# One transformer block on one core: the last row's down tiles, value sums and output turns are put in another order

## The chip, the cores and the metric

The kernel runs on one core of a Trainium2 chip. The metric is the device time of one execution in microseconds (us); less is better. A core has five engines with a queue of instructions each, which run side by side and meet only through semaphores: TensorE (PE in the profile: matmuls, with weight loads as PEld), VectorE (DVE), ScalarE (ACT), GpSimd (POOL), and SyncE (SP), which here only issues DMA transfers.

## The reference

```python
xn = layernorm(x)                              # x is (16, 512, 512)
q, k, v = split(xn @ w_qkv.T + b_qkv)          # 16 heads of 32
attn = softmax(causal(q @ k.T / sqrt(32)))
a = (attn @ v) @ w_out.T + b_out
f = (silu(xn @ gate_w.T * gate_s) * (xn @ up_w.T * up_s)) @ down_w.T * down_s   # hidden width 1408
return x + a + f
```

The sixteen rows of the batch (512 tokens each) are independent. Here a "row" is one of these sixteen.

## The kernel before

All weights stay in SBUF. Every operand that float16 can't hold is split into a high and a low float16 half, so a product takes three matmul groups (high by high, low by high, high by low) where both sides are split, and two where the weights are ternary.

**Tiles.** A row has four token tiles of 128 tokens. Attention is done in 20 chunks (`NCH`), two to each unit of `UNITS`. A unit is a query tile of a group of four heads: `U3` is token tile 3, `U20` tiles 2 and 0, `U1` tile 1 of two head groups at once. The first ten chunks belong to head groups 0 and 1, the last ten to groups 2 and 3. The last unit is a `U1`, so chunks 18 and 19 hold only token tile 1 of head groups 2 and 3; every other part of the attention output is finished by chunk 17.

**Slots.** `period(b, mode)` on each engine runs a row in 20 slots. In slot s, PE computes scores for chunks s and s+1 (if s is even), then two stretches of filling work, the value sums of chunk s-2 (`values`, 16 short matmuls), and a third stretch of filling. DVE takes the row maxima of chunk s (`bank_max`, L1155), ACT the exponents (L855) and the high half (`p_hi`, L865), POOL the low half (`p_lo`, L1244), SP turns both halves with two DMA transposes (L506 high, L508 low) into `p_t`, and PE can then sum the values two slots later. What comes out is summed and normalised on DVE (L1163, L1167, L1173), split into `o_hl` on ACT (L873, `o_hi`) and POOL (L1249, `o_lo`).

**The filling work** is written out by hand in `PLAN`, one string per slot: `d1*4` is four parts of down tile 1, `g` and `u` are gate and up tiles, `q k v` projections of the input, `o` a tile of the output projection of the row before. A down tile (`down_part`) has six parts of 4, 4, 4, 4, 3 and 3 matmuls, 22 in all; an output projection tile (`project`) has three parts of 4. Words 0-1, 2-3 and the rest of a string go to the three stretches of the slot. Results take one of three PSUM banks in turn (`bank_free` waits until the bank's last user was read). `DVE_MID`, `ACT_MID` and `POOL_MID` say in the same way in which slot and place each engine takes the results.

**Row ends.** In a row's slot 18 SP turns the attention output of head groups 0 and 1 (`turn_o(0)`, `turn_o(1)`, L456); groups 2 and 3 are turned in slot 2 of the next row, whose slots 4 and 5 hold the projection. The modes are `first` (row 0), `mid` (a hardware loop over rows 1 to 14), `last` (row 15) and `tail` (what is left of row 15). Before the change, `last` uses `PLAN` without the items of a next row, and `tail` has 7 slots with the output projection alone. In the tail, SP first issues the load of row 15's input as the residual (L472) and turns groups 2 and 3 when all 20 chunks are done. POOL adds the output bias to the residual in four tiles (`b0` to `b3`, L1253) and the scaled down product (`f0` to `f3`, L1259), DVE adds the projection (`combine`, L1088), and SP stores each tile.

The tail of POOL's table begins with these two slots, in which `o_lo` of chunks 18 and 19 stands ahead of the third place:

```python
POOL_MID = [
    "| | b0 b1", "| | b2 b3", "| | f0 f1", "| | f2 f3", ...
```

Of the kernel before, what the change touches and what calls it, by code (L numbers as in the profile page):

```python
# [7 lines left out]
F16 = mybir.dt.float16  # L8
# [5 lines left out]
P = 128  # L14
B, S, D = 16, 512, 512
H, HD = 16, 32
# [60 lines left out]
PLANS = {"none": PLAN_NONE, "first": PLAN_FIRST, "mid": PLAN, "last": PLAN, "tail": PLAN}  # L77
PARTS = dict(v=3, q=3, k=3, r=3, s=3, g=2, u=2, o=3, d=6)
# [3 lines left out]
def has(mode, kind):  # L82
    if kind in "obf":
        return mode != "first"
    if kind in "rsyYxRnl":
        return mode in ("first", "mid")
    return mode != "tail"


TAIL_SLOTS = 7  # L90
# [79 lines left out]
READS = dict(DVE=(DVE_MID, DVE_FIRST), ACT=(ACT_MID, ACT_FIRST), POOL=(POOL_MID, POOL_FIRST))  # L170
# [3 lines left out]
def read_places(engine, mode):  # L174

    places = {}
    for s, text in enumerate(READS[engine][mode == "first"]):
# [82 lines left out]
def block_program(nc, x, w_qkv, gate, up, w_out, down, smalls, b_out, down_s, out):  # L260
    with ExitStack() as ctx:
# [16 lines left out]
        o_hl = sb("o_hl", [P, DC, 2, TT, P], F16)  # L278
# [33 lines left out]
        o_t = region_a[:, :].rearrange("p (c w n) -> p c w n", c=DC, w=2)  # L312
# [39 lines left out]
        def o_dst(s, w):  # L352

            kind, g = UNITS[s // 2]
            cols = slice(2 * HD * (s % 2), 2 * HD * (s % 2) + 2 * HD)
            if kind == "U3":
                return o_hl[:, g, w, 3:4, cols].rearrange("p t (j d) -> p j t d", d=HD)
            if kind == "U20":
                return o_hl[:, g, w, 0:3:2, cols].rearrange("p t (j d) -> p j t d", d=HD)
            return o_hl[:, g:g + 2, w, 1, cols].rearrange("p e (j d) -> p j e d", d=HD)  # L360
# [32 lines left out]
        consts_done = ctx.enter_context(nc.semaphore("consts_done"))  # L393
        bv_split = ctx.enter_context(nc.semaphore("bv_split"))
# [18 lines left out]
        def row_of(b, kind):  # L413
            return b - 1 if kind == "o" else b + 1 if kind in "rs" else b
# [5 lines left out]
        def _(sp):  # L420
# [34 lines left out]
            def turn_o(c, name):  # L455
                sp.dma_start_transpose(o_t[:, c, :, :].rearrange("p w (t n) -> p (w t) n", n=P),  # L456
                                       o_hl[:, c, :, :, :].rearrange("p w t n -> p (w t n)"))\
                  .then_inc(sem[name], 16)

            def period(b, mode):  # L460
                cur, prev, nxt = mode != "tail", mode != "first", mode in ("first", "mid")
                for s in range(NCH if cur else TAIL_SLOTS):
# [15 lines left out]
                    if s in (5, 6) and prev:  # L478
                        for t in range(2 * (s - 5), 2 * (s - 5) + 2):
                            sp.wait_ge(sem["out_added"], at(b - 1, "out_added", t + 1))  # L480
# [37 lines left out]
        def _(pe):  # L518
# [57 lines left out]
            def project(bank, t, k):  # L576
                a, v = [(0, 0), (1, 0), (0, 1)][k]
                toks = slice(t * P, (t + 1) * P)
                for c in range(DC):
                    last = mm(ps[:, bank, :], o_t[:, c, v, toks], weight(OUT, a, c, 0, D),  # L580
                              k == 0 and c == 0, k == 2 and c == DC - 1)
                if k == 2:
                    last.then_inc(sem["proj_ready"], 1)

            def bank_free(b, mode, n):

                user, ago = bank_user(mode, n)
                if user is None:
                    return
                kind, i = user  # L590
                r = row_of(b - ago, kind)
                if kind == "v":
                    pe.wait_ge(sem["v_lo"], at(r, "v_lo", V_COUNT[i]))
                elif kind == "g":
                    pe.wait_ge(sem["gated"], at(r, "gated", i + 1))
                elif kind == "u":
                    pe.wait_ge(sem["hidden"], at(r, "hidden", i + 1))
                elif kind == "o":
                    pe.wait_ge(sem["out_added"], at(r, "out_added", i + 1))
                elif kind == "d":  # L600
# [84 lines left out]
            def period(b, mode):  # L685
                cur, prev, nxt = mode != "tail", mode != "first", mode in ("first", "mid")

                def fill(s, place):
                    for n, k in PLACED[mode].get((s, place), []):
# [26 lines left out]
                        elif kind == "u":  # L716
                            ffn_part(bank, UP, i, k, "up_ready", mode != "first" or i >= UNFLAGGED)
                        elif kind == "d":
                            down_part(b, bank, i, k)
                        else:  # L720
# [178 lines left out]
        def _(dve):  # L899
# [164 lines left out]
            def period(b, mode):  # L1064
# [14 lines left out]
                def scale_down(bank, t):  # L1079
                    dve.wait_ge(sem["down_ready"], at(b, "down_ready", t + 1))  # L1080
# [4 lines left out]
                def combine(bank, t):  # L1085
                    dve.wait_ge(sem["proj_ready"], at(b - 1, "proj_ready", t + 1))
# [5 lines left out]
                def take(s, place):  # L1092
                    for kind, i in READ_PLACES["DVE", mode][s, place]:
# [8 lines left out]
                        elif kind == "d":  # L1102
                            scale_down(bank_at(mode, kind, i), i)
# [94 lines left out]
        def _(pool):  # L1198
# [35 lines left out]
            def period(b, mode):  # L1234
# [16 lines left out]
                def add_bias(t):  # L1251
                    pool.wait_ge(sem["res_loaded"], at(b - 1, "res_loaded", 16))
# [9 lines left out]
                def take(s, place):  # L1262
                    for kind, i in READ_PLACES["POOL", mode][s, place]:
# [8 lines left out]
                        elif kind == "b":  # L1272
                            add_bias(i)
# [51 lines left out]
```

## Time and profile before

| | us |
|---|---|
| median of 3 runs | 1969.26 (1968.77 to 1971.07) |
| the profiled execution | 1970.23 |
| its span, first to last instruction | 1968.5 |
| PE busy | 1894.2 (96% of the span) |
| DVE, ACT, POOL busy | 1347.6, 1294.5, 1361.9 |
| mean granted TensorE clock | 0.988 of full speed |

Busy times are of the profiled execution. What lies around its span is 1.7 us.

### The profile page before, as it was taken

How to read it: one execution, taken by the hardware profiler on the slowest of the kernel's cores; microseconds unless marked ns; L12 is line 12 of the kernel's file. 1: busy time of each engine (PE TensorE's matmuls, PEld its weight loads, DVE VectorE, ACT ScalarE, POOL GpSimd, SP SyncE). 2: the span in 40 equal slices, each digit the busy share in tenths (PEclk: the TensorE clock that was granted, in tenths of full speed). 3: DMA queues.
4: the chain of work that ended last, by engine and by line, in shares of the span. 5: the costliest groups of instructions: out<-in, count | busy, mean ns of one | idle time of the engine just before them, and what ended most of it. 6: DMA issues, size and time to landing. Idle time of an engine off the chain costs nothing.

```text
span 1968.5 us, 48427 instructions
## 1 busy us (share of the span) xinstructions
PE 1894.2 (96%) x15624; PEld 913.2 (46%) x15624; DVE 1347.6 (68%) x3925; ACT 1294.5 (66%) x2315; POOL 1361.9 (69%) x1097
## 2 busy tenths in 40 slices
PE   5879999999999999999999999999999999999995
PEld 2334444444444444444444444444444444444442
DVE  7896676767667676666767666676766767676663
ACT  3776666766667666766766666676676767666662
POOL 1186686766868677687866768676676867668754
PEclk9899999999999999999999999999999999999997
DMA  9248868596776869768586876859677685977855
GB/s 336 38 77 141 156 108 152 112 160 141 121 150 115 152 128 151 145 116 154 109 160 124 153 143 110 158 103 162 134 129 149 116 149 118 157 142 120 149 91 111
DMA packets 840049, 267.89 MB, mean 136 GB/s; under 512 B 812864, under 2 KB 812864, under 8 KB 839232
## 3 DMA queue, kind: packets, MB, share of 16 engines
q1 hardware_dynamic: 839872, 265.15, 71.7%
q8 instruction: 158, 2.59, 0.6%
q14 instruction: 19, 0.16, 0.0%
HBM read 46.94 MB, written 16.78 MB: 32 GB/s over the span
## 4 chain that ended last, share of the span: by engine, by line
PE 80%; DVE 5%; POOL 5%; issue 4%; SPq 3%; DMA 2%; ACT 1%; DVEq 0%; POOLq 0%; ACTq 0%
PE ps L520 80%; POOL phl L1244 2%; DMA p_t<-phl 2%; SPq L442 1%; POOL region_b L1222 1%; DVE memory L938 1%; DVE p L1155 1%; POOL memory L1239 1%; SPq L506 1%; SPq L508 0%; POOL region_a L1227 0%; DVE hidden_tmp L1069 0%; SPq L456 0%; POOL rstd L1218 0%; DVE hidden_tmp L1075 0%
## 5 line engine op out<-in xcount | busy, mean ns | idle before, releaser
L520 PE MATMUL ps<-x_t,memory 128*128 128x512 f16 x4384 | 1004.8, 381 | 9.2 <-DVE memory L938 4.2
L1244 POOL TENSOR_TENSOR phl<-p,phl 128x1024 f16<-128x1024 f32 x320 | 683.0, 2135 | 456.5 <-ACT phl L865 456.4
L855 ACT ACTIVATE p<-p,nmax 128x384 f32<-128x384 f32 (+3 forms) x1024 | 530.1, 557 | 288.7 <-DVE nmax L1155 269.3
L520 PEld LDWEIGHTS ps<-x_t,memory 128*128 128x128 f16 x4384 | 408.0, 98 | 504.7 <-issue 58.3
L1155 DVE CUSTOM_DVE_ANT_0 p<-ps,causal,cst 128x384 f32<-128x384 f32 (+3 forms) x1024 | 515.4, 547 | 97.1 <-PE ps L520 77.0
L865 ACT CAST phl<-p 128x1024 f16<-128x1024 f32 x320 | 334.0, 1044 | 38.4 <-DMA p_t<-phl 22.4
L520 PE MATMUL ps<-memory 128*128 128x512 f16 x1408 | 323.4, 380 | 0.8 <-DVE bout_bc L1007 0.8
L1239 POOL TENSOR_TENSOR memory<-hidden_tmp,memory 128x512 f16<-128x512 f32 x176 | 204.0, 1159 | 69.2 <-ACT memory L827 69.2
L1163 DVE TENSOR_REDUCE ps<-ps 128x132 f32<-128x264 f32 (+1 forms) x320 | 122.0, 381 | 164.0 <-PE ps L520 163.9
L520 PEld LDWEIGHTS ps<-vv,p_t 128*128 128x128 f16 x5120 | 186.8, 96 | 93.0 <-issue 17.4
L520 PE MATMUL ps<-vv,p_t 128*128 128x68 f16 (+1 forms) x5120 | 193.7, 185 | 13.2 <-DMA p_t<-phl 13.0
L520 PEld LDWEIGHTS ps<-memory 128*128 128x128 f16 x1408 | 131.4, 98 | 154.9 <-issue 7.0
L873 ACT CAST o_hl<-o 128x128 f16<-128x128 f32 (+1 forms) x320 | 87.8, 274 | 163.2 <-DVE o L1173 162.3
L520 PE MATMUL ps<-memory,region_a 128*128 128x512 f16 x768 | 176.1, 383 | 10.2 <-DMA region_a<-o_hl 10.2
L1069 DVE SCALAR_TENSOR_TENSOR hidden_tmp<-hidden_tmp,ps 128x512 f32<-128x512 f32 x176 | 120.1, 682 | 86.8 <-ACT hidden_tmp L820 86.3
L520 PE MATMUL ps<-memory,x_t 128*128 128x512 f16 x768 | 173.3, 379 | 0.0
L1025 DVE SCALAR_TENSOR_TENSOR qk<-ps,smalls_in,qk 128x512 f16<-128x512 f32 x128 | 96.0, 750 | 95.5 <-ACT qk L764 95.4
L820 ACT ACTIVATE hidden_tmp<-ps,tanh_scale 128x512 f32<-128x512 f32 x176 | 119.4, 679 | 51.3 <-PE ps L520 46.1
L520 PE MATMUL ps<-qk 32*128 32x128 f16 (+3 forms) x3072 | 134.3, 298 | 5.9 <-DVE nmax L1155 5.9
L764 ACT ACTIVATE qk<-ps,smalls_in 128x512 f16<-128x512 f32 x128 | 87.2, 681 | 75.6 <-PE ps L520 75.6
L1249 POOL TENSOR_TENSOR o_hl<-o,o_hl 128x128 f16<-128x128 f32 (+1 forms) x320 | 125.8, 393 | 11.6 <-ACT o_hl L873 11.6
L1075 DVE SCALAR_TENSOR_TENSOR hidden_tmp<-hidden_tmp,h_scale,ps 128x512 f32<-128x512 f32 x176 | 130.8, 743 | 2.1
(78 smaller groups left out, 1318.6 us busy)
## 6 DMA issues: line engine op xcount, KB each, us to landing
region_b<-x SPq DMA_DIRECT2D x32, 1024.0 KB, 5.8
out<-region_b SPq DMA_DIRECT2D x64, 256.0 KB, 2.5
p_t<-phl SPq DMA_TRANSPOSE x640, 3.1
memory<-w_qkv SPq DMA_DIRECT2D x3, 1024.0 KB, 9.1
memory<-down SPq DMA_DIRECT2D x1, 2816.0 KB, 22.0
memory<-gate SPq DMA_DIRECT2D x1, 2560.0 KB, 9.6
memory<-up SPq DMA_DIRECT2D x1, 2560.0 KB, 16.5
x_t<-region_a SPq DMA_TRANSPOSE x64, 4.0
```

Of the source, the lines that this page charges most:

```text
L520: return nc.tensor.matmul(o, lhsT=l, rhs=r, start=start, stop=stop, skip_group_check=True)
L820: nc.scalar.activation(hidden_tmp[:, f % 2, :], ps[:, bank, :], ACT.Tanh, scale=tanh_scale[:, f:f + 1]).then_inc(sem["tanh_done"], 1)
L855: last = nc.scalar.activation(cols, cols, ACT.Exp, scale=-1.0, bias=nmax[:, s % 2, i:i + 1])
L865: nc.scalar.copy(phl[:, s % 2, 0, :], p32[:, s % 2, :]).then_inc(sem["p_hi"], 1)
L1025: v.scalar_tensor_tensor(out=qk[:, t, side, 1, :], in0=ps[:, bank, :], scalar=bqkv[:, tile:tile + 1], in1=qk[:, t, side, 0, :], op0=ALU.ad ...
L1069: v.scalar_tensor_tensor(out=hidden_tmp[:, f % 2, :], in0=hidden_tmp[:, f % 2, :], scalar=1.0, in1=ps[:, bank, :], op0=ALU.add, op1=ALU.mu ...
L1075: v.scalar_tensor_tensor(out=hidden_tmp[:, f % 2, :], in0=hidden_tmp[:, f % 2, :], scalar=h_scale[:, f:f + 1], in1=ps[:, bank, :], op0=ALU ...
L1155: v.tensor_tensor_reduce(p32[:, s % 2, col:col + w], ps[:, 2 * (s % 2) + jj, col - 512 * jj:col - 512 * jj + w], causal[:, S - w:S], cst[: ...
L1163: v.tensor_reduce(o_sums(n), o_halves(n), AX, ALU.add).then_inc(sem["o_sum"], 1)
L1239: g.tensor_tensor(h_t(1, f), hidden_tmp[:, f % 2, :], h_t(0, f), ALU.subtract)\
L1244: g.tensor_tensor(phl[:, s % 2, 1, :], p32[:, s % 2, :], phl[:, s % 2, 0, :], ALU.subtract)\
L1249: g.tensor_tensor(o_dst(s, 1), o_src(s), o_dst(s, 0), ALU.subtract).then_inc(sem["o_lo"], 1)
```

## The change

1. `PLAN_LAST`: the last row makes down tiles 0 and 1 only, in slots 14 to 19, with 2 parts in each slot where there were 4 to 6. Down tiles 2 and 3 become items `D` of the tail.
2. `PLAN_TAIL`: the tail has three slots instead of seven. Slot 0 is all of D2 and the first part of D3 (the first 16 matmuls of D2 ahead of the value sums of chunk 18). Slot 1 is D3's parts 1 to 4, the value sums of chunk 19, D3's part 5 and projection tile 0. Slot 2 is projection tiles 2, 3 and 1.
3. `o_hl` and `o_t` are laid out by token tile first and half second, with the tiles in the order 0, 2, 3, 1, in all rows. In the tail, groups 2 and 3 are turned in two steps: tiles 0, 2, 3 as soon as chunk 17 is split, tile 1 once chunk 19 is. Only projection tile 1 waits for the second step. The other rows turn whole groups as before.
4. Row 15's residual load moves from the tail to slot 8 of the last row, and the four bias additions (`c0` to `c3`) to POOL's slots 10 to 13.
5. DVE scales d0 in slot 17 and d1 in slot 19; D2 and D3 follow the outputs of chunks 18 and 19. POOL's tail is `f0 f1`, o_lo of chunk 18, `f2`, o_lo of chunk 19, `f3`.

```diff
+PLAN_LAST = PLAN[:14] + ["u10*2 d0*2", "d0*2", "d0*2", "d1*2", "d1*2", "d1*2"]
+PLAN_TAIL = ["D2*6 D3*1", "D3*5 o0*3", "o2*3 o3*3 o1*3"]
+PLANS = {"none": PLAN_NONE, "first": PLAN_FIRST, "mid": PLAN, "last": PLAN_LAST, "tail": PLAN_TAIL}
+TILE_ORDER = [0, 2, 3, 1]
-TAIL_SLOTS = 7
+TAIL_SLOTS = len(PLAN_TAIL)
...
+DVE_LAST = DVE_MID[:16] + ["| | |", "d0 | | |", "| | |", "| | | d1"]
+POOL_LAST = list(POOL_MID)
+POOL_LAST[10:14] = [text + f" c{t}" for t, text in enumerate(POOL_MID[10:14])]
+DVE_TAIL = ["| | | D2", "| | | D3", "o0 o2 o3 o1 | | |"]
+ACT_TAIL = ["| | | |"] * 3
+POOL_TAIL = ["f0 f1 | | f2", "| | f3", "| |"]
...
-        o_hl = sb("o_hl", [P, DC, 2, TT, P], F16)
+        o_hl = sb("o_hl", [P, DC, TT, 2, P], F16)
...
+            def turn_o_tiles(tiles, done):
+
+                for c in (2, 3):
+                    sp.dma_start_transpose(o_t[:, c, tiles, :, :].rearrange("p t w n -> p (t w) n"),
+                                           o_hl[:, c, tiles, :, :].rearrange("p t w n -> p (t w n)"))\
+                      .then_inc(done, 16)
...
-                    if s == 0 and prev:
-                        if cur:
-                            sp.wait_ge(sem["ln_lo"], at(b, "ln_lo", TT))
-                        else:
-                            sp.wait_ge(sem["out_stored"], at(b - 2, "out_stored", 16 * TT))
+                    if s == 0 and prev and cur:
+                        sp.wait_ge(sem["ln_lo"], at(b, "ln_lo", TT))
                         sp.dma_start(res[:, :, :], x[b - 1].rearrange("(t p) n -> p t n", p=P))\
                           .then_inc(sem["res_loaded"], 16)
-                    if s == 2 and prev:
+                    if s in (0, 1) and not cur:
+                        sp.wait_ge(sem["o_lo"], at(b - 1, "o_lo", NCH - 2 + 2 * s)).then_inc(wait_over["sp"], 1)
+                        if s == 0:
+                            turn_o_tiles(slice(0, TT - 1), sem["turned23"])
+                        else:
+                            turn_o_tiles(slice(TT - 1, TT), turned_last)
+                    if s == 2 and prev and cur:
...
+                    if s == 8 and cur and prev and not nxt:
+                        sp.wait_ge(sem["out_stored"], at(b - 1, "out_stored", 16 * TT))
+                        sp.dma_start(res[:, :, :], x[b].rearrange("(t p) n -> p t n", p=P))\
+                          .then_inc(sem["res_loaded"], 16)
...
+                            elif i == 1 and k == 0 and not cur:
+                                pe.wait_ge(turned_last, 32)
                             project(bank, i, k)
```

## Rows read from the trace of the kernel before

**Rows 1.** Engines by stretch: start:end, length, busy times (instructions), granted clock, DMA share, GB/s.
```profile
1709.00:1817.00 108.00, 107.74 (x893) 51.90 (x892) 74.36 (x222) 72.21 (x133) 80.08 (x64) 1.00 0.73 134
...
1911.00:1921.77 10.77, 10.77 (x99) 5.28 (x98) 5.94 (x19) 5.92 (x11) 5.83 (x5) 1.00 0.70 100
...
1931.98:1938.42 6.44, 0.60 (x16) 0.52 (x17) 1.02 (x4) 1.29 (x2) 2.75 (x3) 0.63 0.99 191
```

**Rows 2.** TensorE in order of time: start, length, what, idle before it.
```profile
1910.34 5.34 PE L520 MATMUL ps<-memory 128*128 128x512 f16 x24
...
1917.36 0.83 PE L520 MATMUL ps<-qk 32*128 32x128 f16 x24
...
1924.62 0.60 PE L520 MATMUL ps<-vv,p_t 128*128 128x68 f16 x16
...
1928.12 3.18 PE L520 MATMUL ps<-memory 128*128 128x512 f16 x14
1931.98 0.60 PE L520 MATMUL ps<-vv,p_t 128*128 128x68 f16 x16 [0.68 <-DMA p_t<-phl]
1938.42 0.84 PE L520 MATMUL ps<-vv,p_t 128*128 128x68 f16 x16 [5.84 <-DMA p_t<-phl]
1940.96 0.84 PE L520 MATMUL ps<-vv,p_t 128*128 128x68 f16 x16 [1.70 <-DMA p_t<-phl]
1951.98 13.27 PE L520 MATMUL ps<-memory,region_a 128*128 128x512 f16 x48 [10.18 <-DMA region_a<-o_hl]
```

**Rows 3.** SyncE's queue in order of time: start, length of issuing, what.
```profile
1928.36 2.20 SPq L508 DMA_TRANSPOSE p_t<-phl  x1
1930.75 2.60 SPq L456 DMA_TRANSPOSE region_a<-o_hl  x2
...
1937.69 1.28 SPq L508 DMA_TRANSPOSE p_t<-phl  x1
1939.03 0.57 SPq L472 DMA_DIRECT2D region_b<-x  x1
1947.39 2.62 SPq L456 DMA_TRANSPOSE region_a<-o_hl  x2
```

**Rows 4.** The chain that ended last: start, length, what.
```profile
1934.89 3.40 DMA p_t<-phl
```

**Rows 5.** GpSimd in order of time, slot 15 and the tail.
```profile
1914.86 2.12 POOL L1244 TENSOR_TENSOR phl<-p,phl 128x1024 f16<-128x1024 f32 x1 [0.58 <-ACT phl L865]
...
1940.69 0.43 POOL L1249 TENSOR_TENSOR o_hl<-o,o_hl 128x128 f16<-128x128 f32 x1 [5.14 <-ACT o_hl L873]
1944.43 2.48 POOL L1253 TENSOR_TENSOR region_b<-region_b,bout_bc 128x512 f32<-128x512 f32 x2 [3.31 <-DMA region_b<-x]
1946.87 0.43 POOL L1249 TENSOR_TENSOR o_hl<-o,o_hl 128x128 f16<-128x128 f32 x1
```

**Rows 6.** Engines by stretch, as Rows 1, for the clock.
```profile
1933.50:1951.98 18.48, 1.68 (x33) 1.50 (x34) 1.93 (x7) 0.89 (x3) 10.02 (x10) 0.50 0.70 154
1951.98:1957.40 5.42, 5.42 (x13) 1.87 (x14) 0.10 (x1) 0.00 (x0) 2.63 (x3) 0.50 0.00 0
1957.40:1965.30 7.90, 7.84 (x36) 3.38 (x34) 2.17 (x4) 0.00 (x0) 0.00 (x0) 0.99 0.26 100
...
103.50:107.50 4.00, 3.95 (x11) 1.50 (x12) 4.00 (x8) 1.04 (x3) 3.06 (x2) 0.58 0.95 102
117.50:121.00 3.50, 2.33 (x24) 1.29 (x24) 3.43 (x6) 3.45 (x6) 2.23 (x2) 1.00 0.31 61
```

**Rows 7.** VectorE in order of time, slots 15 and 17.
```profile
1912.87 0.08 DVE L1155 DVE_READ_ACCUMULATOR2_ANT nmax<- 128x1 f32 x1
...
1924.83 0.75 DVE L1081 SCALAR_TENSOR_TENSOR ffn_out<-ps,cst,downs_bc 128x512 f32<-128x512 f32 x1 [0.49 <-PE ps L520]
```

**Rows 8.** TensorE early in row 0, two waits.
```profile
103.55 5.30 PE L520 MATMUL ps<-x_t,memory 128*128 128x512 f16 x16 [3.03 <-DVE lo_flag L933]
...
117.71 1.89 PE L520 MATMUL ps<-x_t,memory 128*128 128x512 f16 x8 [1.93 <-DVE hidden_tmp L1069]
```

More of the change, by code:

```diff
@@ L76 @@
 ]
-PLANS = {"none": PLAN_NONE, "first": PLAN_FIRST, "mid": PLAN, "last": PLAN, "tail": PLAN}
-PARTS = dict(v=3, q=3, k=3, r=3, s=3, g=2, u=2, o=3, d=6)
+PLAN_LAST = PLAN[:14] + ["u10*2 d0*2", "d0*2", "d0*2", "d1*2", "d1*2", "d1*2"]
+PLAN_TAIL = ["D2*6 D3*1", "D3*5 o0*3", "o2*3 o3*3 o1*3"]
+PLANS = {"none": PLAN_NONE, "first": PLAN_FIRST, "mid": PLAN, "last": PLAN_LAST, "tail": PLAN_TAIL}
+PARTS = dict(v=3, q=3, k=3, r=3, s=3, g=2, u=2, o=3, d=6, D=6)
+TILE_ORDER = [0, 2, 3, 1]
 def has(mode, kind):
@@ L84, in has @@
         return mode != "first"
+    if kind == "D":
+        return mode == "tail"
     if kind in "rsyYxRnl":
@@ L87, in has, with o_rank @@
     return mode != "tail"
-TAIL_SLOTS = 7
+TAIL_SLOTS = len(PLAN_TAIL)
+def o_rank(mode, t):
+    return TILE_ORDER.index(t) if mode == "tail" else t
 BEFORE = {"first": "none", "mid": "mid", "last": "mid", "tail": "last"}
@@ L169 @@
 ]
-READS = dict(DVE=(DVE_MID, DVE_FIRST), ACT=(ACT_MID, ACT_FIRST), POOL=(POOL_MID, POOL_FIRST))
+DVE_LAST = DVE_MID[:16] + ["| | |", "d0 | | |", "| | |", "| | | d1"]
[4 more added lines that the diff above has]
+POOL_TAIL = ["f0 f1 | | f2", "| | f3", "| |"]
+TABLES = {
+    "first": dict(DVE=DVE_FIRST, ACT=ACT_FIRST, POOL=POOL_FIRST), "mid": dict(DVE=DVE_MID, ACT=ACT_MID, POOL=POOL_MID),
+    "last": dict(DVE=DVE_LAST, ACT=ACT_MID, POOL=POOL_LAST), "tail": dict(DVE=DVE_TAIL, ACT=ACT_TAIL, POOL=POOL_TAIL),
+}
 STEPS = dict(DVE=4, ACT=5, POOL=3)
@@ L176, in read_places @@
     places = {}
-    for s, text in enumerate(READS[engine][mode == "first"]):
+    for s, text in enumerate(TABLES[mode][engine]):
         parts = text.split("|")
@@ L413, in row_of @@
         def row_of(b, kind):
-            return b - 1 if kind == "o" else b + 1 if kind in "rs" else b
+            return b - 1 if kind in "oD" else b + 1 if kind in "rs" else b
         def qk_count(kind, t):
@@ L455, in turn_o @@
             def turn_o(c, name):
[L456 to L457 removed]
+                sp.dma_start_transpose(o_t[:, c, :, :, :].rearrange("p t w n -> p (t w) n"),
+                                       o_hl[:, c, :, :, :].rearrange("p t w n -> p (t w n)"))\
                   .then_inc(sem[name], 16)
+            def turn_o_tiles(tiles, done):
[3 more added lines that the diff above has]
+                      .then_inc(done, 16)
             def period(b, mode):
@@ L477, in period @@
                         turn_o(3, "turned23")
-                    if s in (5, 6) and prev:
-                        for t in range(2 * (s - 5), 2 * (s - 5) + 2):
-                            sp.wait_ge(sem["out_added"], at(b - 1, "out_added", t + 1))
+                    if s in ((5, 6) if cur else (1, 2)) and prev:
+                        half = s - (5 if cur else 1)
+                        for n in range(2 * half, 2 * half + 2):
+                            t = n if cur else TILE_ORDER[n]
+                            sp.wait_ge(sem["out_added"], at(b - 1, "out_added", n + 1))
                             sp.dma_start(out[b - 1].rearrange("(t p) n -> p t n", p=P)[:, t, :], res[:, t, :])\
                               .then_inc(sem["out_stored"], 16)
+                    if s == 8 and cur and prev and not nxt:
+                        sp.wait_ge(sem["out_stored"], at(b - 1, "out_stored", 16 * TT))
+                        sp.dma_start(res[:, :, :], x[b].rearrange("(t p) n -> p t n", p=P))\
+                          .then_inc(sem["res_loaded"], 16)
                     if s == 8 and nxt and prev:
@@ L577, in project @@
                 a, v = [(0, 0), (1, 0), (0, 1)][k]
-                toks = slice(t * P, (t + 1) * P)
                 for c in range(DC):
-                    last = mm(ps[:, bank, :], o_t[:, c, v, toks], weight(OUT, a, c, 0, D),
+                    last = mm(ps[:, bank, :], o_t[:, c, TILE_ORDER.index(t), v, :], weight(OUT, a, c, 0, D),
                               k == 0 and c == 0, k == 2 and c == DC - 1)
@@ L590, in bank_free @@
                 kind, i = user
-                r = row_of(b - ago, kind)
+                r, m = row_of(b - ago, kind), BEFORE[mode] if ago else mode
                 if kind == "v":
```

33 lines of the change are left out of this document (19 added, 14 removed).

## The prediction

> **What bounds the kernel now.** I read the stretches first. In a whole row of the loop TensorE is busy 107.74 of 108 us [rows 1]: a row costs what its matmuls cost, and the new layout of `o_hl` and `o_t` changes the size of no instruction there (each write keeps its strides and count, each turn its 1024 columns, each weight load its 128 contiguous columns), so rows 0 to 14 are costed at nothing, and TensorE's fullness would hide small differences. What can change is the end. I took TensorE in order of time next [rows 2]: it works without a gap until slot 18 [rows 1, 2], then waits 0.68, 5.84 and 1.70 us for the turned probabilities of chunks 17, 18 and 19 and 10.18 us for the turned output: 18.4 us in which it has nothing to do, although 22 of the down matmuls of slots 18 and 19 (d3) could have stood there, and d2's too. Third, the chain and the two queues that feed those waits. SyncE issues six transposes back to back between 1930.75 and 1939.0 [rows 3], with the DMA engines 0.99 busy [rows 1], and a transpose lands 3.4 us after it is issued [rows 4]. Then it loads the residual; GpSimd waits 3.31 us for that load and adds two bias tiles before it splits chunk 19 [rows 5], so the last turns leave at 1947.39 [rows 3]; with chunk 18's time from the start of its values to its split, 2.7 us, they could have left at 1943.7. Last, the clock: from 1933.5 on TensorE is granted half speed (1.2 GHz instead of 2.4), and keeps it for the first 5.4 us of the projection [rows 6].
>
> **Unit prices.** 24 down matmuls take 5.34 us and 14 take 3.18 [rows 2], so one costs 0.216 us at full clock. The 48 of the projection took 13.27 us where 48 x 0.216 is 10.4: the half clock cost 2.9 us there. A `values` is 0.60 us at full clock and 0.84 at half [rows 2].
>
> **Step 1, slots 14 to 19 with 44 matmuls fewer.** That is 9.5 us of TensorE, but only what the attention's own chain leaves open can be won. In slot 15 TensorE now has 8 matmuls after 1910.34 instead of 24: it is at the values of chunk 13 at 1912.1 and done at 1912.7. The scores of chunks 16 and 17 also need the maxima of chunk 15, read at 1912.87 to 1912.95 [rows 7], so they start at 1913.05 instead of 1917.36 [rows 2]: 4.3 us earlier. From here TensorE no longer sets the pace. The low half of chunk 15 is made by GpSimd from 1914.86 to 1916.98 [rows 5], as before; turned and landed 3.4 us later that is 1920.45, so the values of chunk 15 run at 1920.5 instead of 1924.62: 4.1 earlier. Chunks 16 and 17 pass through the same operations with the same lengths; d0's scaling (0.75 us [rows 7]) now stands ahead of chunk 17's maxima, where d2's stood behind them, which costs a few tenths. I take the low transpose of chunk 17 at 1924.55 instead of 1928.36 [rows 3]: 3.8 us earlier. Behind it SyncE has the same six transposes at the same spacing, so chunk 17's values run at 1928.2 and chunk 18's at 1934.6 instead of 1938.42 [rows 2]. Step 1 is worth 3.8 us, not 9.5. From below: nothing, if the transposes of slots 16 to 18 crowd one another; from above 4.3.
>
> **Step 2, down tiles 2 and 3 in the waits.** After chunk 17's values at 1928.8 TensorE does 16 matmuls of D2 (3.5 us), is done at 1932.3 and waits until 1934.6; these are free. After chunk 18's values (to 1935.2) come 25 matmuls, 5.4 us, before the values of chunk 19, which start at 1940.6. Their data would be there at 1940.96 - 3.8 = 1937.2, so here work is put ahead of a value sum that was ready, by 3.4 us. It costs nothing as long as tile 1's turn is not late: TensorE is then simply busy. The values end at 1941.2; 3 more matmuls of D3, 0.65, and the projection can start at 1941.9, if tiles 0, 2 and 3 are turned. Their turn needs only chunk 17 and follows chunk 19's low transpose, at 1933.9 + 1.3; two transposes of 2.6 us together [rows 3] and the landing give about 1940. In time by almost 2 us.
>
> **Step 3, the projection.** 48 matmuls at full clock are 10.4 us: it ends at 1952.25 instead of 1965.26. Tile 1 is last, at 1941.9 + 36 x 0.216 = 1949.7. From the start of a value sum to its split is 2.7 us (1938.42 to 1941.12 [rows 2, 5]), so chunk 19 is split at 1943.3; at the full-size price for its two small transposes (1947.39 to 1951.98 is 4.6 us [rows 2, 3]) they land at 1947.9. In time by 1.8 us. GpSimd has `f0 f1` done before chunk 18 comes and `f2` (1.2 us, after D2's scaling) between 18 and 19, so o_lo of chunk 19 waits for nothing. Behind SyncE's wait for it stand only the stores, which are needed later.
>
> **Step 4, the residual's load and bias.** In slot 8 the load waits for the stores of slots 5 and 6, with the probabilities' transposes queued behind; every row of the loop does this with the next input, and TensorE stays full [rows 1]. The four additions are 1.24 us each [rows 5] in slots where the loop's rows also have the normalisation, so they are hidden; without that cover 5 us. The end behind the last matmul (3.2 us) does not change.
>
> **Sum at full clock.** 1965.26 - 1952.25 = 13.0 us: 3.8 of step 1; 6.3 between chunk 18's values and the projection (13.6 us before, now 0.6 + 5.4 + 0.6 + 0.65 = 7.3); 2.9 in the projection itself.
>
> **The clock.** The last 2.9 us are the doubtful part. TensorE will be thinner than before: the slots from 15 on hold 8 down matmuls per 4 us, with waits of some 2.8 us before chunk 17's values and 2.3 before chunk 18's. After a wait of 3.03 us early in the kernel the clock was at half (0.58 over the next 4 us), after one of 1.93 us it stayed at 1.00 [rows 6, 8]; here the waits lie between. A drop in slots 17 to 19 costs almost nothing, as half-speed matmuls only fill the waits. A drop that lasts past 1934.6 costs up to what the projection paid, 2.9. I take half, 1.3, as both neighbours are equally near; the ends are 0 and 2.9. The Trainium skill (TensorE: Matmul & The Clock Gate, HAM oscillation) speaks against this change here: short bursts of matmuls with waits for data between them are throttled again at each wait, and every burst starts cold. By it the sum would be 10.1 instead of 11.7; the early rows agree with it for one wait and not for the other.
>
> So 11.7 us less. The profiled execution (span and 1.7 us around it) would be 1970.23 - 11.7 = 1958.5; the median of the runs lies 0.97 below that execution, so **1957.6**.
>
> **Rivals.**
> - **A, the clock stays low into the projection.** For: the waits above, and the drop at 1933.5, only 0.9 us after chunk 17's values. Gain 13.0 - 2.9 = 10.1, time 1959.2; this lies in the forecast's own range.
> - **B, the slots keep their old pace.** Step 1 gives nothing because SyncE's transposes, not TensorE, set the slots. For: 2.20 us for issuing one at 1928.36 [rows 3], where the one at 1937.69 took 1.28, and the six in a row. Against: TensorE was full in slots 15 and 16 and its value sums waited for no DMA there [rows 1, 2]. Gain 9.2, with the clock low 6.3: 1960.1 to 1963.
> - **C, tile 1's turn is late.** The value sum of chunk 19 is held behind 15 matmuls of D3. If splitting and turning took 9.1 us instead of 7.3, the projection would wait. At worst another 2 us: gain 9.7, 1959.6.
> - **D, slower.** TensorE, thinned in slot 15, falls to half clock and stays there to the end. From slot 15 it has 8 + 6 + 22 + 44 + 48 = 128 long matmuls, 0.21 us dearer each: 27 us on TensorE, of which the waits in the slots take 7 or so and the rest exceeds the gain of 13.0 by 7: 1976. It decides from 62 half-clock matmuls on the path. Against: a full 5.4 us brought the clock back [rows 6], and cold matmuls would fill the slots.
> - **E, no effect.** The projection waits as long as before because something else holds its turn, e.g. the residual's load. Against: the load is gone from the tail, the order of SyncE's queue is plain.
>
> **Chances.** The forecast, with the clock nearer to full speed than to A, 0.42; A 0.30; B 0.12; C 0.06; D 0.03; E 0.03; more than 13.5 gained (issue gaps that shrink) 0.04. The forecast's own range is 1956.2 to 1959.2. Two in ten left out: 1955.0 to 1962.0. 0.2% is 3.9 us, about what a measurement of this kernel can tell from no change: faster by more than that 0.94, within it 0.03, slower 0.03.
>
> **What would show it.** Right: values of chunk 15 some 4 us earlier, chunk 18's near 1934.6, the D matmuls without idle time between chunk 18's values and the projection's last matmul, that one near 1952 to 1955. Wrong: idle time of TensorE before the projection or before its last 12 matmuls (C); the spacing of slots 16 to 18 as before (B); matmuls of 0.43 us through D3 and most of the projection (A, D). A difference in the loop's rows would mean that the layout is not neutral.

## The result, and the profile after

The changed kernel takes 1955.2 us (median of 4 runs, 1953.38 to 1956.67) against 1970.16 for the kernel before, timed beside it: ratio 0.9922, with a 95% interval of 0.9905 to 0.994. That is 15.4 us less, with 11.8 to 18.7 inside the interval. Forecast were 11.7 us, with 7.3 to 14.3 as the range that follows from its two ends: the direction was right, and the gain lies above that range, where the prediction ("more than 13.5 gained") had put a chance of 0.04. In time, 1955.2 us lies below the forecast's own range of 1956.2 to 1959.2. Where the gain came from is mostly as forecast; what was missed is told by terms further down.

Runs of one kernel differ by up to 6.5 us. The traces, one execution of each kernel, show where such differences can arise: in the twelve of them, row 1 starts to turn its probabilities at 192.9 to 195.6 us, and from there to slot 14 of the last row it is 1710.1 to 1714.6 us, so time differs both while the weights are prepared and in the loop. (For the kernels before and after, it is 1711.1 and 1711.2.) In what follows I therefore use a second measure, the **end stretch**: from the start of the scores of chunks 14 and 15 of the last row (the last place up to which all kernels do nearly the same) to the end of the span. It is one execution per kernel too. Before: 1968.5 - 1905.67 = 62.8 us. After: 1954.6 - 1906.58 = 48.0. So the end gained 14.8 us in the profiled executions, and this one reached slot 14 0.9 us later than the one before.

TensorE in order of time in the changed kernel, beside [rows 2]:

```profile
1906.58 0.83 PE L562 MATMUL ps<-qk 32*128 32x512 f16 x12
...
1914.01 0.84 PE L562 MATMUL ps<-qk 32*128 32x128 f16 x24 [0.43 <-DVE nmax L1200]
...
1921.42 0.60 PE L562 MATMUL ps<-vv,p_t 128*128 128x68 f16 x16 [2.12 <-DMA p_t<-phl]
...
1923.35 2.86 PE L562 MATMUL ps<-memory 128*128 128x512 f16 x8
...
1928.29 0.60 PE L562 MATMUL ps<-vv,p_t 128*128 128x68 f16 x16 [0.24 <-DMA p_t<-phl]
1928.74 3.61 PE L562 MATMUL ps<-memory 128*128 128x512 f16 x16
1933.88 0.60 PE L562 MATMUL ps<-vv,p_t 128*128 128x68 f16 x16 [1.53 <-DMA p_t<-phl]
1934.33 5.55 PE L562 MATMUL ps<-memory 128*128 128x512 f16 x25
1939.72 0.61 PE L562 MATMUL ps<-vv,p_t 128*128 128x68 f16 x16
1940.17 0.81 PE L562 MATMUL ps<-memory 128*128 128x512 f16 x3
1940.82 10.52 PE L562 MATMUL ps<-memory,region_a 128*128 128x512 f16 x48
```

From chunk 18's values (1933.88) on TensorE has no gap: D2, D3, the values of chunk 19 and all four projection tiles stand end to end. The waits of 5.84, 1.70 and 10.18 us before [rows 2] are one of 1.53. In the thinned slots ahead TensorE now has waits that were not there, the longest of 2.12 us. The projection takes 10.52 us where it took 13.27.

The engines by stretch, beside [rows 1, 6]:

```profile
1709.00:1817.00 108.00, 107.94 (x904) 52.25 (x903) 73.49 (x220) 72.55 (x132) 80.16 (x64) 1.00 0.72 135
1921.90:1925.30 3.40, 3.40 (x34) 1.49 (x31) 2.37 (x11) 1.89 (x5) 2.39 (x2) 0.50 1.33 126
1925.30:1933.90 8.60, 6.83 (x59) 3.14 (x58) 4.14 (x17) 4.89 (x10) 5.26 (x5) 1.00 0.97 188
1933.90:1951.40 17.50, 17.44 (x108) 8.20 (x108) 5.51 (x12) 0.60 (x2) 5.53 (x6) 1.00 0.51 96
```

The row of the loop is as full as before. The clock did fall, behind the wait of 2.12 us, and stood at half for the scores and 8 down matmuls of slot 18; it was back before the tail, where it stayed at 1.00.

SyncE's queue, beside [rows 3], and the chain that ended last, beside [rows 4]:

```profile
1924.70 1.38 SPq L550 DMA_TRANSPOSE p_t<-phl  x1
1926.27 2.61 SPq L482 DMA_TRANSPOSE region_a<-o_hl  x2
1929.06 1.23 SPq L548 DMA_TRANSPOSE p_t<-phl  x1
1930.41 1.26 SPq L550 DMA_TRANSPOSE p_t<-phl  x1
1931.86 1.23 SPq L548 DMA_TRANSPOSE p_t<-phl  x1
1933.38 1.23 SPq L550 DMA_TRANSPOSE p_t<-phl  x1
1934.73 10.00 SPq L489 DMA_TRANSPOSE region_a<-o_hl  x4
```

```profile
1924.70 3.46 DMA p_t<-phl
...
1930.41 3.33 DMA p_t<-phl
...
1933.88 17.48 PE ps L562 x108
```

Measured from the start of the end stretch, chunk 17's low transpose is issued at 18.1 us (22.7 before), the turns of groups 0 and 1 at 19.7 (25.1), chunk 18's values at 27.3 (32.75), the projection at 34.2 (46.3).

### The profile page after: what moved, and what is told of

The parts are those of the page before. It is cut to its first block, busy times and chain, and to the rows that moved or that the text cites. A ratio compares the mean times of both kernels' runs of the same rounds, so it can differ in the third digit from the quotient of the medians.

```text
span 1954.6 us, 48431 instructions
## 1 busy us (share of the span) xinstructions
PE 1892.8 (97%) x15624; PEld 912.5 (47%) x15624; DVE 1347.6 (69%) x3925; ACT 1294.4 (66%) x2315; POOL 1362.8 (70%) x1097
## 4 chain that ended last, share of the span: by engine, by line
PE 75%; POOL 7%; DVE 6%; issue 4%; SPq 3%; DMA 2%; ACT 1%; DVEq 0%; POOLq 0%; ACTq 0%
PE ps L562 75%; POOL phl L1289 3%; DMA p_t<-phl 2%; SPq L468 2%; POOL region_b L1267 2%; DVE memory L983 1%; DVE p L1200 1%; POOL memory L1284 1%; SPq L548 1%; DVE hidden_tmp L1114 1%; POOL region_a L1272 1%; POOL rstd L1263 0%; SPq L550 0%; DVE hidden_tmp L1120 0%; DVE vareps L1065 0%
## 5 line engine op out<-in xcount | busy, mean ns | idle before, releaser
L910 ACT CAST phl<-p 128x1024 f16<-128x1024 f32 x320 | 334.0, 1044 | 39.6 <-DMA p_t<-phl 23.4
L562 PE MATMUL ps<-vv,p_t 128*128 128x68 f16 (+1 forms) x5120 | 193.0, 185 | 10.5 <-DMA p_t<-phl 10.4
L865 ACT ACTIVATE hidden_tmp<-ps,tanh_scale 128x512 f32<-128x512 f32 x176 | 119.5, 679 | 52.3 <-PE ps L562 46.3
```

The costliest lines, as they stand in the source:

```text
L562: return nc.tensor.matmul(o, lhsT=l, rhs=r, start=start, stop=stop, skip_group_check=True)
L865: nc.scalar.activation(hidden_tmp[:, f % 2, :], ps[:, bank, :], ACT.Tanh, scale=tanh_scale[:, f:f + 1]).then_inc(sem["tanh_done"], 1)
L910: nc.scalar.copy(phl[:, s % 2, 0, :], p32[:, s % 2, :]).then_inc(sem["p_hi"], 1)
```

## The experiments

Each is read by its end stretch; the ratio to the kernel before, with its interval, stands beside it where there is one; the two kernels without a ratio (more warm-up, chunk 19 first) ran once. A matmul in them is one of 512 columns.

| kernel | end stretch, us | ratio of times |
|---|---|---|
| before | 1968.5 - 1905.67 = 62.8 | |
| before, clock kept | 1966.7 - 1906.45 = 60.2 | 0.9993 [0.9983, 1.0003] |
| before, early residual | 1963.1 - 1903.92 = 59.2 | 0.9978 [0.9968, 0.9987] |
| before, more warm-up | 1970.5 - 1908.69 = 61.8 | |
| changed | 1954.6 - 1906.58 = 48.0 | 0.9922 [0.9905, 0.994] |
| changed, down tiles back | 1959.1 - 1905.87 = 53.2 | 0.9956 [0.9942, 0.997] |
| changed, whole turn | 1962.0 - 1905.78 = 56.2 | 0.9968 [0.9956, 0.9979] |
| changed, late residual | 1954.1 - 1904.56 = 49.5 | 0.995 [0.9935, 0.9966] |
| changed, chunk 19 first | 1959.4 - 1906.99 = 52.4 | |
| changed, d0 behind | 1955.1 - 1907.06 = 48.0 | 0.9933 [0.9918, 0.9948] |
| slots filled | 1952.8 - 1904.27 = 48.5 | 0.993 [0.9917, 0.9944] |
| slots filled, kept warm | 1953.6 - 1907.48 = 46.1 | 0.9925 [0.9911, 0.9938] |

### What the half clock cost before

```diff
+                def junk(n):
+                    pe.wait_ge(sem["s_max"], at(b - 1, "s_max", PIECES_UNTIL[-1]))
+                    for _ in range(n):
+                        mm(ps[:, 0, :], x_t[:, 0, 0, 0:P], weight(QKV, 0, 0, 0, D), True, True)
...
+                    if not cur and s == 0:
+                        junk(24)
+                    if not cur and s == 2:
+                        junk(40)
```

> The kernel before, with 24 + 40 extra matmuls of 512 columns in the tail (into a PSUM bank that nobody reads any more): 24 before the value sums of chunk 18, 40 after those of chunk 19, where TensorE waits 5.8 and 10.2 us. Nothing else changes. The end stretch, from the start of the scores of chunks 14 and 15 of the last row to the last instruction, is 62.8 us before and 48.0 after. Theory (the half clock cost the projection 2.9 us, and the change got that back): the first 12 matmuls of the projection take 0.216 us instead of 0.43, the end stretch is 59.9 to 60.2. Rival (the first matmuls are slow for another reason, such as fetching what the transposes just wrote): 62.8, with the clock shown at full.

The tail of TensorE in this kernel:

```profile
1942.32 9.96 PE L520 MATMUL ps<-memory,x_t 128*128 128x512 f16 x40
1952.92 10.52 PE L520 MATMUL ps<-memory,region_a 128*128 128x512 f16 x48 [0.63 <-DMA region_a<-o_hl]
```

The projection starts at 46.5 us of the end stretch (46.3 before) and takes 10.52 us instead of 13.27. So 2.6 to 2.8 of the 14.8 us are the clock alone, and matmuls that compute nothing win them as well. The ratio to before can't tell 2.6 us from nothing; the trace can.

### The residual's load and bias alone

The edit is step 4 of the change, put on the kernel before.

```diff
-                        else:
-                            sp.wait_ge(sem["out_stored"], at(b - 2, "out_stored", 16 * TT))
...
+                    if s == 8 and cur and prev and not nxt:
+                        sp.wait_ge(sem["out_stored"], at(b - 1, "out_stored", 16 * TT))
+                        sp.dma_start(res[:, :, :], x[b].rearrange("(t p) n -> p t n", p=P))\
+                          .then_inc(sem["res_loaded"], 16)
...
+POOL_LAST[10:14] = [text + f" c{t}" for t, text in enumerate(POOL_MID[10:14])]
+POOL_TAIL = ["| |", "| |"] + POOL_MID[2:]
```

> The kernel before with step 4 alone: the residual's load in slot 8 of the last row, the bias in slots 10 to 13. Theory: chunk 19 is split 3.7 us earlier (GpSimd no longer waits for the load and adds two bias tiles first), the turns and the projection follow, the end stretch is 62.8 - 3.7 = 59.1. Rival (the load in slot 8 delays the turns of the probabilities in the last row, or the addition of the down tiles becomes the wait): 60.5 or more, or TensorE with idle time in slots 8 to 13.

GpSimd and TensorE in the tail:

```profile
1939.21 0.43 POOL L1256 TENSOR_TENSOR o_hl<-o,o_hl 128x128 f16<-128x128 f32 x1 [5.15 <-ACT o_hl L880]
1941.74 0.42 POOL L1256 TENSOR_TENSOR o_hl<-o,o_hl 128x128 f16<-128x128 f32 x1 [2.10 <-ACT o_hl L880]
```

```profile
1946.81 13.05 PE L527 MATMUL ps<-memory,region_a 128*128 128x512 f16 x48 [6.50 <-DMA region_a<-o_hl]
```

Chunk 19 is split 2.5 us behind chunk 18, where before it was 6.2 [rows 5]; TensorE's wait shrinks by 3.7. The other way round, with step 4 taken out of the changed kernel:

```diff
+                    if s == 0 and not cur:
+                        sp.wait_ge(sem["out_stored"], at(b - 2, "out_stored", 16 * TT))
+                        sp.dma_start(res[:, :, :], x[b - 1].rearrange("(t p) n -> p t n", p=P))\
+                          .then_inc(sem["res_loaded"], 16)
...
-POOL_TAIL = ["f0 f1 | | f2", "| | f3", "| |"]
+POOL_TAIL = ["| | b0 b1", "| | b2 b3", "f0 f1 f2 f3 | |"]
```

> The changed kernel with step 4 undone: the residual's load is issued in the tail, ahead of the turns of tiles 0, 2 and 3, and the bias is added in the tail, two tiles behind the split of chunk 18 and two behind that of chunk 19, then the four additions of the down tiles. Theory (with the change TensorE is the bound of the tail, and GpSimd has some slack): what cost 3.6 us in the kernel before costs 0.5 to 2 us here, since only VectorE's last combinations wait for GpSimd; end stretch 48.5 to 50. Rival (the early load is needed for the whole gain): 51.5 or more.

GpSimd's bias add, and TensorE's projection, each in order of time:

```profile
1938.98 2.49 POOL L1297 TENSOR_TENSOR region_b<-region_b,bout_bc 128x512 f32<-128x512 f32 x2 [4.78 <-DMA region_b<-x]
```

```profile
1940.34 10.52 PE L561 MATMUL ps<-memory,region_a 128*128 128x512 f16 x48 [1.50 <-DMA region_a<-o_hl]
```

It costs 1.5 us: the load goes ahead of the turns on the DMA engines, and the projection waits 1.50 us for them (GpSimd's own delay is hidden by the projection; I had expected the cost only there, at VectorE's last additions). Not all of the 1.5 need be the load's: in this trace an instruction fetch also falls into the issuing of the first of those turns, which takes 2.38 us, where in the changed kernel the same one, with a fetch near its end, takes 1.31. The same step is worth 3.6 us on one kernel and 1.5 on the other, so the parts of the change don't add.

### The two down tiles back in the slots, and the turn made whole

```diff
-PLAN_LAST = PLAN[:14] + ["u10*2 d0*2", "d0*2", "d0*2", "d1*2", "d1*2", "d1*2"]
-PLAN_TAIL = ["D2*6 D3*1", "D3*5 o0*3", "o2*3 o3*3 o1*3"]
+PLAN_LAST = PLAN
+PLAN_TAIL = ["", "", "o0*3 o2*3 o3*3 o1*3"]
```

> The changed kernel with down tiles 2 and 3 back in slots 15 to 19 of the last row (the old plan); the turns by token tiles, the order of the projection and the early residual stay. Theory: TensorE fills slots 15 to 19 as before, so the value sums come as late as before; the turns of tiles 0, 2 and 3 are issued right behind the last probabilities and land some 5 us later, the projection starts at 39 us of the end stretch, cold, and takes 13.3: 55.5 in all, so about half of the 14.8 us comes from moving the two tiles. Rival (the turns are what counts, and the tiles only fill time): 50 or less.

```diff
-                        sp.wait_ge(sem["o_lo"], at(b - 1, "o_lo", NCH - 2 + 2 * s)).then_inc(wait_over["sp"], 1)
-                        if s == 0:
-                            turn_o_tiles(slice(0, TT - 1), sem["turned23"])
-                        else:
-                            turn_o_tiles(slice(TT - 1, TT), turned_last)
+                        if s == 1:
+                            sp.wait_ge(sem["o_lo"], at(b - 1, "o_lo", NCH)).then_inc(wait_over["sp"], 1)
+                            turn_o(2, "turned23")
+                            turn_o(3, "turned23")
```

> The changed kernel with groups 2 and 3 turned whole once chunk 19 is split; all else stays, also the 25 down matmuls ahead of the value sums of chunk 19. Theory: the split of chunk 19 is done at 35.6 us of the end stretch, the turns take 4.6, the projection starts at 40.3 instead of 34.2: 54.1, and up to 57 if the clock drops in the 5.5 us wait. Rival (the turn is hidden by the down matmuls anyway): 48 to 49.

The projection on TensorE, in order of time, with the down tiles back and then with the whole turn:

```profile
1943.54 12.34 PE L562 MATMUL ps<-memory,region_a 128*128 128x512 f16 x48 [1.34 <-DMA region_a<-o_hl]
```

```profile
1945.92 12.81 PE L561 MATMUL ps<-memory,region_a 128*128 128x512 f16 x48 [5.85 <-DMA region_a<-o_hl]
```

With the down tiles back, the end is 5.2 us longer than with the change; I expected 7.5. Two things made the difference: the projection came at 37.7 us of the stretch instead of 39, and it lost 1.9 us to the half clock instead of 2.9. With the whole turn it is 8.2 us longer: 5.85 of waiting and 2.3 of clock. So both moves are needed, and each is worth more than its own wait, since the wait also takes the clock down. With the down tiles back, chunk 18's values come at 32.7 us, as in the kernel before, and not at 27.3: moving the tiles out makes the slots end earlier. How much earlier they can end is the next question.

### What sets the slots

I had put d0's scaling on the path, at a few tenths of a microsecond.

```diff
-DVE_LAST = DVE_MID[:16] + ["| | |", "d0 | | |", "| | |", "| | | d1"]
+DVE_LAST = DVE_MID[:16] + ["| | |", "| | | d0", "| | |", "| | | d1"]
```

> The changed kernel with VectorE's scaling of d0 (0.75 us) moved from ahead of chunk 17's maxima to the end of slot 17. Theory (that scaling stands on the chain values of chunk 14, maxima of chunk 17, low half of 17, its turn, and with it all later turns): the low transpose of chunk 17 and the values of chunk 18 come 0.65 us earlier, the end stretch is 47.3. Rival (SyncE's queue or TensorE sets these): 47.95.

Nothing was won: chunk 17's low transpose is issued 18.1 us into the end stretch in both kernels. ScalarE in this kernel shows why:

```profile
1919.33 1.96 ACT L900 ACTIVATE p<-p,nmax 128x128 f32<-128x128 f32 x4
1921.84 1.04 ACT L910 CAST phl<-p 128x1024 f16<-128x1024 f32 x1 [0.55 <-DMA p_t<-phl]
```

and so does its chain:

```profile
1918.47 3.29 DMA p_t<-phl
...
1921.84 1.05 ACT phl L910
...
1922.96 2.14 POOL phl L1289
...
1925.18 1.38 SPq L550
```

Chunk 17's exponents are ready 0.55 us before its high half can be written, because the buffer `phl` is read by chunk 15's transposes until they land. From chunk 15 to chunk 17 the work runs in a ring: high half (1.05), low half (2.14), transpose and landing (3.3), high half two chunks later; with the gaps, 6.7 us (1915.13 to 1921.84 in this kernel). In the changed kernel the chain does run through d0's scaling:

```profile
1917.60 0.31 DVE ps L1208
...
1918.30 0.73 DVE ffn_out L1126
```

But there chunk 17's exponents end and chunk 15's transposes land within 0.1 us of each other, so taking either away alone wins nothing.

### The instruction fetch

Chunk 17's low transpose took 2.20 us to issue before [rows 3] and 1.38 after. In the trace of before, a 16 KB fetch of instructions stands in the DMA queues in that time:

```profile
q8 instruction: 1, 0.02, 3.2%
...
p_t<-phl SPq DMA_TRANSPOSE x1, 3.5
```

(The DMA queues from 1928.5 to 1930.5.) It starts at 1929.06. In the changed kernel it comes at 1923.84, while SyncE waits for the low half, and the issue starts at 1924.70.

```diff
-PE_PAD = 38
+PE_PAD = 52
```

> The kernel before with 52 instead of 38 tiny warm-up matmuls at the very start of TensorE's program, where it waits anyway: 28 instructions more ahead of everything. In the trace of before, the 16 KB fetch of instructions at 1929.06 falls into the issuing of chunk 17's low transpose, which takes 2.20 us; in the changed kernel the fetch falls between two issues and that transpose takes 1.38 us. Theory (the fetch is what makes the issuing long, and its place follows from how many instructions TensorE has run): the fetch comes about 1.5 us earlier against the slots, the issuing of that transpose is 1.3 to 1.8 us instead of 2.20, and the end stretch shortens by the same, to 61.9 to 62.4 from 62.75. Rival (the long issue comes from the transposes in flight, which are the same): 2.2 us and 62.75, wherever the fetch is.

SyncE's queue in this kernel, with the low transposes of chunk 17 and of chunk 19, and then TensorE's projection:

```profile
1931.38 1.82 SPq L508 DMA_TRANSPOSE p_t<-phl  x1
...
1940.33 1.26 SPq L508 DMA_TRANSPOSE p_t<-phl  x1
```

```profile
1954.70 12.60 PE L520 MATMUL ps<-memory,region_a 128*128 128x512 f16 x48 [10.26 <-DMA region_a<-o_hl]
```

The fetch moved by 0.4 us (from 23.4 to 23.0 us into the end stretch), not by 1.5, and the issue became 0.38 shorter. The other 0.6 to 0.7 us of the 1.0 won are the projection's, 12.60 instead of 13.27, that is the clock, and with one trace of each kernel they can't be put down to the edit (see the last section).

Over all twelve kernels the issue of chunk 17's low transpose took 2.20, 2.10, 2.49, 2.23 and 1.82 us with a fetch in it, and 1.23 to 1.40 without one. For the other transposes that is not the whole rule. The twelve end stretches have 230 transposes, 27 of them with a fetch inside the issuing: 19 of these took 1.8 to 2.5 us to issue and 8 only 1.23 to 1.33. In seven of the 8 the fetch came 0.9 us or later into the issue, in the long ones within 0.72; the eighth, with the fetch at 0.65, is met below. Of the 203 others three took 1.59, 1.71 and 2.06 us, each right behind one with a fetch in it, and none of the rest more than 1.43. So no long issue stands without a fetch in it or in the one before, but a fetch does not make every issue long. Which instructions bring the fetch, and why it holds an issue up, is not shown.

### Chunk 19 first

`-*4` leaves the first two places of a slot empty, so that all of D3 follows the value sums.

```diff
-PLAN_TAIL = ["D2*6 D3*1", "D3*5 o0*3", "o2*3 o3*3 o1*3"]
+PLAN_TAIL = ["D2*6", "-*4 D3*6 o0*3", "o2*3 o3*3 o1*3"]
```

> The changed kernel with the value sums of chunk 19 right after D2, ahead of all of D3 (22 matmuls), instead of behind 19 of them. Theory (TensorE is the bound from chunk 18's values on, so a value sum may wait behind down matmuls for nothing): TensorE now waits about 1.1 us for chunk 19's turned halves, and the end stretch is 48.9 to 49.1 instead of 47.95. Rival (the turn of tile 1 was close to being the bound, so an earlier split helps): 47.95 or less.

TensorE around chunk 19's values in this kernel, and then the landing that they wait for, from its chain:

```profile
1934.71 1.46 PE L566 MATMUL ps<-memory 128*128 128x512 f16 x6
1938.80 0.60 PE L566 MATMUL ps<-vv,p_t 128*128 128x68 f16 x16 [2.63 <-DMA p_t<-phl]
1939.24 6.59 PE L566 MATMUL ps<-memory 128*128 128x512 f16 x22
```

```profile
1933.81 4.85 DMA p_t<-phl
```

The direction is as expected and the size is not: 4.4 us instead of 1.1. The wait is 2.63 us because chunk 19's transpose takes 4.85 us from issue to landing, not the 3.3 that I had reckoned with (an instruction fetch falls into that time too; in the changed kernel itself the same transpose took 4.6). Behind the wait the clock is at half: 22 matmuls need 6.4 us up to the projection instead of 4.75. Holding a ready value sum behind down matmuls was therefore not free but right: it hides a late landing and keeps the clock. This is one execution, but both parts can be seen in it: 2.63 us of waiting and 1.7 us of half clock make 4.3 of the 4.4.

### Filling the waits that are left

```diff
-PLAN_LAST = PLAN[:14] + ["u10*2 d0*2", "d0*2", "d0*2", "d1*2", "d1*2", "d1*2"]
-PLAN_TAIL = ["D2*6 D3*1", "D3*5 o0*3", "o2*3 o3*3 o1*3"]
+PLAN_LAST = PLAN[:14] + ["u10*2 d0*2", "d0*2", "d0*2", "d1*4", "d1*2 d2*2", "d2*4"]
+PLAN_TAIL = ["D3*6", "-*4 o0*3", "o2*3 o3*3 o1*3"]
...
-DVE_LAST = DVE_MID[:16] + ["| | |", "d0 | | |", "| | |", "| | | d1"]
-DVE_TAIL = ["| | | D2", "| | | D3", "o0 o2 o3 o1 | | |"]
+DVE_LAST = DVE_MID[:16] + ["| | |", "| | | d0", "| | |", "| | | d1 d2"]
+DVE_TAIL = ["| | | D3", "| | |", "o0 o2 o3 o1 | | |"]
```

> The previous one, and down tile 2 put back into the last row, spread over the places where TensorE still waits: d1 with 4 parts in slot 17, its last 2 and 2 of d2 in slot 18, 4 of d2 in slot 19; the tail has D3 alone, around the value sums of chunk 18, and nothing between the values of chunk 19 and the projection. Theory (after chunk 17's transposes the turns of tiles 0, 2 and 3 are the next bound: issued behind chunk 19's low transpose, landing some 4.6 us later): the projection starts 31.5 to 32.5 us into the end stretch instead of 34.2, with TensorE waiting about 2 us before it; 45.5 to 46.5 in all, and 0.5 to 1.5 more if the clock drops in that wait. Rival (the work in slots 17 to 19 delays the chain itself): 47.5 or more, with chunk 18's values later than 26.7 us.

Of this kernel, SyncE's issue of chunk 18's low transpose, and TensorE's last rows:

```profile
1928.17 2.04 SPq L554 DMA_TRANSPOSE p_t<-phl  x1
```

```profile
1935.05 0.60 PE L566 MATMUL ps<-vv,p_t 128*128 128x68 f16 x16 [0.82 <-DMA p_t<-phl]
1937.33 12.21 PE L566 MATMUL ps<-memory,region_a 128*128 128x512 f16 x48 [1.68 <-DMA region_a<-o_hl]
```

The projection starts at 33.1 us instead of 34.2, later than the 31.5 to 32.5 expected: here the fetch falls into chunk 18's low transpose, which takes 2.04 us. The 1.2 us won are more than lost again to the half clock (12.21 us against 10.52), and the end stretch is 48.5 us, 0.5 longer than with the change and above the 45.5 to 46.5 (at most 1.5 more) expected. Extra matmuls keep it up:

```diff
+                    if not cur and s < 2:
+                        junk(3)
...
+                    if not cur and s == 1:
+                        junk(7)
```

> The kernel with filled slots once more, and 13 extra matmuls of 512 columns in the tail, into a PSUM bank that nobody reads any more: 3 ahead of the value sums of chunk 18, 3 ahead of those of chunk 19 and 7 ahead of the projection, where TensorE waited 0.9, 0.8 and 1.7 us. Theory (the filled kernel won 1.2 us up to the projection and lost 1.7 in it to the half clock): the projection starts 33.1 us into the end stretch as in that kernel, its matmuls take 0.216 us from the first on, and the end stretch is 46.7 to 46.9, 1.1 less than with the change. Rival (the clock falls all the same, or the extra matmuls delay a value sum): 48 or more.

TensorE's last rows in this kernel:

```profile
1938.23 1.67 PE L566 MATMUL ps<-memory,x_t 128*128 128x512 f16 x7
1939.83 10.52 PE L566 MATMUL ps<-memory,region_a 128*128 128x512 f16 x48
```

and SyncE's issue of chunk 18's low transpose, with the DMA queues from 1931.27 to 1932.6:

```profile
1931.27 1.26 SPq L554 DMA_TRANSPOSE p_t<-phl  x1
...
q8 instruction: 1, 0.02, 4.5%
```

The end stretch is 46.1 us, 1.9 less than with the change, and some 0.7 less than expected: the projection starts at 32.35 us, not 33.1, because chunk 18's low transpose took 1.26 us to issue instead of 2.04, although a fetch fell into it here as well (at 1931.92, 0.65 us into the issue; in the filled kernel at 0.55). That part is luck and not the extra matmuls' doing, as they all come later. What they did is the projection at 10.52 us instead of 12.21. This is the shortest end of all; its ratio, 0.9925, can't be told from the change's 0.9922, because the spread of the start is larger than 1.9 us.

## Why the prediction came out as it did

By terms, in us of the end stretch:

| term | forecast | measured |
|---|---|---|
| step 1, up to chunk 18's values | 3.8 | 32.75 - 27.3 = 5.45 |
| from there to the projection | 6.3 | 13.56 - 6.94 = 6.6 |
| the projection | 2.9 - 1.3 = 1.6 | 13.27 - 10.52 = 2.75 |
| sum | 11.7 | 14.8 |

- **Step 1, the failed term.** "I take the low transpose of chunk 17 at 1924.55 instead of 1928.36: 3.8 us earlier", and the same 3.8 for chunk 18's values; measured 5.45. The scores of chunks 16 and 17 and the values of chunk 15 came where I had put them (7.4 and 14.8 us into the stretch, forecast 7.4 and 14.8). What failed are the two steps behind that. First, I carried the 4.1 us of chunk 15's values over to chunk 17, less a few tenths for d0's scaling. But chunk 17's maxima stand behind VectorE's reading of chunk 14's values, for which the prediction has no line. In the chain of the kernel before:

```profile
1921.80 0.31 DVE ps L1163
...
1922.63 0.35 DVE p L1155
```

This reading stands at 16.1 us of the end stretch before and at 11.0 in the changed kernel (1917.60): 5.1 us earlier. d0's scaling takes back 0.5 of it, and the transpose was issued at 18.1 us instead of 22.7, 4.6 earlier; the forecast's place was 18.9. Second, "the same six transposes at the same spacing" was wrong by 0.9: from that issue to chunk 18's values it was 10.06 us before and 9.18 after, 0.8 of it because the 2.20 us of issuing that I read in [rows 3] were 1.38 here, where no instruction fetch fell into it. Together the two are the 1.65 us, and my upper bound of 4.3 excluded the truth. The first is argued from the two chains, with no run of its own.
- **Step 2** held: 25 matmuls ahead of chunk 19's values cost nothing, the turns of tiles 0, 2 and 3 were in time, and the whole-turn and chunk-19-first experiments show what else would have come (8.2 and 4.4 us). The order even earned something I had not seen, by covering a landing of chunk 19's transpose that took 4.6 us and not 3.3.
- **Step 3, the turn of tile 1** held: TensorE had no gap before its last 12 matmuls. Rival C did not occur.
- **Step 4** held: no wait in slots 8 to 13, and 3.7 us in the kernel before. The loop's rows are unchanged (107.94 of 108 us busy).
- **The clock.** "I take half, 1.3": measured 0. The fall came, in slot 18, where the forecast called it nearly free, and it was. Keeping the clock gave 2.6 us in the kernel before, so the price was nearly right (2.75 instead of 2.9, as 48 matmuls at full clock take 10.52 us and not 10.4) and the half was wrong. I had compared the waits alone; after the fall the clock was back at 1925.3, ahead of chunk 18's values, and the one wait left behind that, 1.53 us, did not take it down. The Trainium skill (TensorE: Matmul & The Clock Gate, HAM oscillation) tells of a kernel whose every burst starts cold behind its wait for data; the waits there are of some 3 to 5 us, which the prediction did not say, and the new kernel has none so long. The kernel before agrees with it: behind 5.84 and 10.18 us of waiting its matmuls ran at half clock. In the changed kernel the clock fell behind the wait of 2.12 us and not behind those of 0.63, 0.24 and 1.53; before, it fell 1.1 us after the last work. As a price for every burst the rule would have been too high here.
- **Rivals B and D** did not occur; A did not either, though the down-tiles-back, whole-turn, chunk-19-first and filled kernels each paid 1.7 to 2.3 us for matmuls at half clock behind a wait.
- **The range.** It was cut at 14.3 us of gain. With 13.0 at full clock as the sum of sure terms, only 1.3 was left for every term being too small, while 5.7 was left for the other side. The bounds from the rows should have been as open to a gain: 2.20 us against 1.28 for the same instruction stood in [rows 3], and I used it only as an argument for a rival.

What each part is worth, by taking it out of the changed kernel: the two-step turn 8.2, the moved down tiles 5.2, the early residual 1.5 us. Their sum, 14.9, is near 14.8 by chance: put on the kernel before, the residual alone gives 3.6. The two-step turn's 8.2 holds 2.3 of clock, the down tiles' 5.2 holds 1.8.

## What to carry to other kernels

When a kernel ends in a chain of transfers, look for work that needs none of them and put it where the engine waits: it pays twice where an idle TensorE would drop its clock, and matmuls that compute nothing can show (or be) that second part. Split the last transfer by what its readers need first, and let the part that finishes last be read last. Before an instruction's duration is carried into a sum, compare it with its like: one that is longer than the others of its line has met something, and what it met may not move with it.

## What was not expected of the hardware

- Issuing a DMA transpose of 128 x 1024 float16 takes 1.23 to 1.4 us, and mostly 1.8 to 2.5 when a 16 KB fetch of instructions falls into it (19 of 27 cases; the other 8 took 1.23 to 1.33). Of the turns of the probabilities in the end stretches, those without a fetch between issue and landing landed in 3.0 to 3.6 us, but for one of 4.64; with one, 38 of 62 took 4.0 to 5.2.
- The clock's fall does not follow the length of the wait alone: it fell behind 2.12 us, stayed up through 1.5, and fell 1.1 us into a wait that went on. In one kernel with the same slots (the whole turn) it did not fall in slot 18 at all: the 8 matmuls there took 1.90 us instead of 2.86.
- Nor does it come at a fixed place. Four kernels (before, early residual, down tiles back, more warm-up) wait 5.6 to 5.9 us for chunk 18's probabilities; the clock fell 1.1, 3.8, 4.2 and 3.1 us after the last work, and the projection took 13.27, 13.05, 12.34 and 12.60 us. So a difference of up to 0.9 us between two end stretches can be the clock's moment alone. That 14 more tiny matmuls at the very start brought 0.7 us in this way, as the one trace has it, is not shown.
